# Two PSUM banks for the second attention's projections, and expert outputs added into a stored x by the scatters

## The chip, the cores and the metric

The kernel runs on one core of one Trainium2 chip. The metric is device time in microseconds, lower is better. The kernel before takes 1861.11 us (median of 3 runs, 1853.59 to 1872.67).

## The reference

x has 32 batches of 128 tokens, 256 values each (4096 tokens). Two layers follow one another; each adds an attention and a mixture of experts to x:

```python
x = x + tanh(g_xattn[0]) * L0_xattn(layernorm(x), ctx, ctx, ...)      # 16 heads of 16, with biases
x = x + tanh(g_ffn[0])   * L0_ffn(layernorm(x), ...)                  # 8 experts, top 2, 1024 hidden, relu
x = x + tanh(g_xattn[1]) * L1_xattn(layernorm(x), ctx, ctx, mask)     # causal and padding masks, no W_O
x = x + tanh(g_ffn[1])   * L1_ffn(layernorm(x), ...)                  # 8 experts, top 2, 512 hidden, silu * up
```

In both expert layers a token's output is the sum over its two experts of gate times expert(x). All of it is fp32.

## The kernel before

**Stages.** The program goes through attention 0, experts 0, attention 1, experts 1 and a last combination. x stays in SBUF (tile X) throughout. PE multiplies fp32 as three products of rounded halves (`three`, L371): high by high, high by low, low by high (sources of L373 to L375). So each operand is needed twice: ACT writes the rounded high half and DVE or POOL subtracts it from the whole to get the low half.

**Attention.** Each engine runs its own list in the order of a step counter s, from -21 to 146. A unit is four heads of one batch (128 units); its scores, transposes and products with V sit at fixed steps. A group is four batches (8 groups, 16 steps each). For each group PE also does the transposes of the normalised x ("xt", L416), the projections q, k and v, and for the routing the transposes "lt" (L464), the logits "lg" (L471) and the ranks "rk" (L477, L478). All of these write the one PSUM bank `BK`. `uses_bk` (L323) lists them in order, and `before` makes each wait (`bank_free`, L346) until the one ahead of it has been read out: by DVE for xt, q, k (L755, L763, L773), lg and rk (L797), by ACT for v and lt. The bank `BO_` serves the output projection of attention 0 and is not used in attention 1.

**Routing.** DVE picks two experts per token, their gates (tile GA, times tanh(g_ffn) in tile GT) and the row of each in a memory area sorted by expert. POOL scatters each normalised token twice into `xs_scr` (L1157). A row has 256 values and one more, the number of its place in `ys_scr`: token number plus 4096 for the second choice. Unused rows carry the number 16384.

**Experts.** 39 tiles of 256 rows run per layer, the first 8 of them the first tile of each expert; the number of further tiles per expert is only known on the chip, and tiles left over repeat the last one. Per tile SP fetches rows (L1216) and four parts of weights (L1196) into U1; ACT makes high halves (`act_w`, L650), and POOL (parts 0 and 3) and DVE (parts 1 and 2) the low ones (`low_w`, L1060). PE's order is: up-projection of tile i, transposes of the rows of tile i+1, down-projection of tile i-1. POOL's order per tile (`pool_experts`, L1170) is low half 3 of tile i-1, then `pool_y` of tile i-2, then low half 0 of tile i+1, which the up-projection of tile i+1 needs first. `pool_y` (L1160) waits until the second scatter of the tile before has landed, then issues two indirect DMAs of 128 rows each into `ys_scr` (L1167). In layer 0 DVE adds the bias b2 and writes the output tile `yo` (L1075), in layer 1 ACT copies it (`act_y`, L663). The rows of the next tile are transposed on PE, rounded by ACT (L656) and subtracted by DVE (`dve_turn_x`, L1062); DVE does this after the low halves of the hidden values (L1081 in layer 0, L1083 in layer 1).

**Between the layers and at the end.** `experts_out` (L360) waits for the last scatters. In attention 1 SP loads two outputs per batch from `ys_scr` (L1258) and DVE adds each times its gate to X (L935, L937), ahead of the statistics of the layer norm. After experts 1 SP loads the outputs in 16 DMAs (L1323), DVE does the same sum in 64 instructions (L1356), and ACT's queue writes the result (L1340).

Of the kernel before, what the change touches and what calls it, by code (L numbers as in the profile page):

```python
# [23 lines left out]
ROW = D + 1  # L24
# [20 lines left out]
def constants():  # L45
# [10 lines left out]
    for k in range(2):  # L56
        for b in range(B):
            c[:, C_TOK + k * B + b] = k * T + b * S + p
# [78 lines left out]
def program(nc, A):  # L137
    ctx = ExitStack()
    with ctx:
# [10 lines left out]
        ys_d = [nc.dram_tensor(n, (2 * T, D), F32, kind="Internal").ap() for n in ("ys_scr", "ys1_scr")]  # L150
# [10 lines left out]
        U2 = sb("U2", [128, W0N])  # L161
# [12 lines left out]
        xi = sb("xi", [128, 4, 2], I32)  # L174
        b1s = sb("b1s", [128, 2, 8])
# [19 lines left out]
        GT = sb("GT", [128, 2, 2, B])  # L195
# [30 lines left out]
        YF = [u[:, i * 2048:(i + 1) * 2048].rearrange("p (k g d) -> p k g d", k=2, g=G) for u in (U1, U2, U3) for i in range(2)]  # L226
        YL = U4[:, 0:8 * D].rearrange("p (r k d) -> p r k d", r=4, k=2)
# [6 lines left out]
        oview = A["out"].rearrange("b s d -> s b d")  # L234
# [22 lines left out]
        d_yl = [mark(f"d_yl{r}", [b for b in range(B) if b % 2 == r], 16) for r in range(2)]  # L257
# [8 lines left out]
        d_yf = [mark(f"d_yf{r}", [(g, k) for g in range(NG) if g % 6 == r for k in range(2)], 16) for r in range(6)]  # L266
        d_out = mark("d_out", range(NG), 16)
# [21 lines left out]
        v_yl = mark("v_yl", range(B))  # L289
# [9 lines left out]
        a_y = mark("a_y", [k for k in tile2 if k[0] == 1])  # L299
        m_y = (v_y, a_y)  # L300
# [3 lines left out]
        v_yf = mark("v_yf", range(NG))  # L304
# [35 lines left out]
        before = {}  # L340
# [9 lines left out]
        def banks_out(w, L):  # L350

            w.wait_ge(*a_p[L, NU - 1])
            w.wait_ge(*a_pt[L, NU - 1])
            w.wait_ge(*v_on[L, B - 1])
            w.wait_ge(*a_v[L, NG - 1, 1])
            w.wait_ge(*v_rk[(L,) + PARTS[-1].key])
            if L == 0:
                w.wait_ge(*v_xup[0, B - 1])

        def experts_out(w, L):  # L360

            w.wait_ge(*m_dn[L, NT - 1, 1])
            w.wait_ge(*m_y[L][L, NT - 1, 1])
# [13 lines left out]
        def pe_proj(e, L, wi, src, m):  # L377
            ms = slice(m * 128, m * 128 + 128)
            for t in range(2):
                ins = three(e, BK[:, :], (WR[:, wi, 0, t, ms], WR[:, wi, 1, t, ms]), (src[:, 0, t], src[:, 1, t]), t == 0, t == 1)  # L380
            return ins

        def pe_attention(e, w, L):
            if L == 1:
                experts_out(w, 0)
            for s in range(FIRST, LAST):
# [24 lines left out]
                for t in range(2):  # L411
                    if (g := grp(s, X0[t])) is not None:
                        w.wait_ge(*v_ln1[L, g])
                        bank_free(w, L, "xt", g, t)
                        for j in range(G):
                            ins = e.transpose(BK[:, j * 128:(j + 1) * 128], XN[:, j, t * 128:(t + 1) * 128], ident)  # L416
                        ins.then_inc(*m_xt(L, g, t))
                for m in range(2):
                    if (g := grp(s, Q0[m])) is not None:
# [37 lines left out]
                for p in PARTS:  # L457
                    k = (L,) + p.key
                    for t in range(2):
                        if s == p.lt[t]:  # L460
                            w.wait_ge(*v_xr[k])
                            bank_free(w, L, "lt", p.key, t)
                            for j in range(p.lo, p.hi):
                                ins = e.transpose(BK[:, j * 128:(j + 1) * 128], xr(p.g)[:, 0, j, t * 128:(t + 1) * 128], ident)  # L464
                            ins.then_inc(*m_lt(*k, t))
                    if s == p.e1:
                        w.wait_ge(*a_lt[k + (1,)])
                        bank_free(w, L, "lg", p.key)
                        for j in range(p.lo, p.hi):
                            for t in range(2):  # L470
                                ins = e.matmul(BK[:, j * E:(j + 1) * E], LT[:, t, j * 128:(j + 1) * 128], rw[:, L, t, :], start=t == 0, stop=t == 1)  # L471
                        ins.then_inc(*m_lg(*k))
                    if s == p.rk:
# [3 lines left out]
                        e.matmul(BK[:, 0:p.n * E], cst[:, C_UT:C_UT + 128], sv, start=True, stop=True)  # L477
                        e.matmul(BK[:, 32:32 + p.n * E], cst[:, C_ONE:C_ONE + 128], sv, start=True, stop=True).then_inc(*m_rk(*k))  # L478
# [928 lines left out]
```

## Time and profile before

| what | value |
|---|---|
| runs | 1853.59, 1872.67, 1861.11 us; median 1861.11 |
| profiled execution | 1846.52 us, its span 1844.7 us |
| PE busy | 1653.7 us (90%) |
| weight loads of PE | 1564.0 us (85%) |
| DVE, ACT, POOL busy | 1225.1 (66%), 1198.9 (65%), 791.0 us (43%) |
| mean granted clock of PE | 0.94 |
| DMA | 265.59 MB, 144 GB/s mean |
| chain that ended last | PE 83%, DVE 7%, DMA 3%, issue 2%, POOL 2%, ACT 2% |

Times are us from the start of the span. Attention 0 runs to about 480, experts 0 to 937, attention 1 from about 962 (after the last scatters) to 1438, experts 1 to 1799, the last combination to the end. Busy time of PE is that of modelled matmul ends. "issue" is time in which an engine waited for nothing that the profile shows. A wait is put down to the releaser that came last.

### The profile page before, as it was taken

The numbers are of one execution on the slowest core, as the hardware profiler recorded it, in microseconds if no ns is written. First come the engines' busy times: TensorE is split into PE (matmuls) and PEld (weight loads), VectorE is DVE, ScalarE is ACT, GpSimd is POOL, SyncE is SP. The second block draws the span as 40 slices with busy tenths as digits, with TensorE's granted clock in tenths as the row PEclk, the third lists the DMA queues.
The fourth block names the chain that finished last, engine by engine and source line by source line (L and its number), as shares of the span: only waits on it lengthen the run. The fifth ranks groups of instructions, "written<-read, shape, count | busy, mean of one in ns | idle before, by whom it ended". The sixth has DMA issues, their size and how long they took to land.

```text
span 1844.7 us, 36398 instructions
## 1 busy us (share of the span) xinstructions
PE 1653.7 (90%) x12444; PEld 1564.0 (85%) x12444; DVE 1225.1 (66%) x2877; ACT 1198.9 (65%) x2795; POOL 791.0 (43%) x877
## 2 busy tenths in 40 slices
PE   3999999998599999999976999999995799999990
PEld 2899899897499999999964888888894799999990
DVE  2566665656577777777756677778757566666655
ACT  1667666664488888888843666656662577777760
POOL 2123332224366666666651113333323366666650
PEclk9999998997699999999997999999996799999995
DMA  2212221113677777788742222222221677777758
GB/s 94 47 47 68 66 57 48 48 46 98 168 229 231 231 226 232 229 232 236 225 152 69 63 64 85 79 77 83 57 73 45 206 233 235 230 227 232 231 179 281
DMA packets 209514, 265.59 MB, mean 144 GB/s; under 512 B 28225, under 2 KB 155461, under 8 KB 209201
## 3 DMA queue, kind: packets, MB, share of 16 engines
q1 hardware_dynamic: 189840, 222.36, 41.9%
q0 software_dynamic: 13632, 35.13, 5.2%
q10 hardware_dynamic: 5856, 5.77, 1.0%
q8 instruction: 99, 1.62, 0.4%
q14 instruction: 87, 0.70, 0.1%
HBM read 202.89 MB, written 45.69 MB: 135 GB/s over the span
## 4 chain that ended last, share of the span: by engine, by line
PE 83%; DVE 7%; DMA 3%; issue 2%; POOL 2%; ACT 2%; SPq 1%; DVEq 0%; POOLq 0%; ACTq 0%
PE ps L373 20%; PE ps L375 20%; PE ps L374 20%; PE ps L490 11%; PE ps L393 6%; PE ps L500 2%; PE ps L471 2%; PE ps L409 1%; POOL xs_scr L1157 1%; DMA U<-ys_scr 1%; PE ps L464 1%; PE ps L416 1%; DVE X L1356 1%; DMA xs_scr<-U,PI 1%; DMA ys_scr<-U,xi 1%
## 5 line engine op out<-in xcount | busy, mean ns | idle before, releaser
L1060 POOL TENSOR_TENSOR KXR<-U,KXR 128x1024 fp32r<-128x1024 f32 (+1 forms) x156 | 334.5, 2144 | 306.1 <-ACT KXR L650 305.2
L373 PE MATMUL ps<-QR,KXR 128*128 128x256 f32 x1248 | 355.3, 285 | 8.4 <-DVE QR L1064 8.4
L374 PE MATMUL ps<-QR,KXR 128*128 128x256 f32 x1248 | 354.7, 284 | 0.0
L375 PE MATMUL ps<-QR,KXR 128*128 128x256 f32 x1248 | 354.3, 284 | 0.0
L650 ACT ACTIVATE KXR<-U 128x1024 fp32r<-128x1024 f32 (+1 forms) x312 | 287.7, 949 | 78.0 <-PE ps L375 63.7
L561 ACT ACTIVATE U<-ps,mx 128x128 f32<-128x128 f32 x1024 | 291.7, 379 | 5.7 <-DVE mx L914 5.0
L490 PEld LDWEIGHTS ps<-VA,U 128*128 128x128 f32 x2048 | 267.4, 198 | 9.7
L914 DVE TENSOR_REDUCE mx<-ps 128x4 f32<-128x512 f32 x256 | 175.3, 685 | 126.9 <-PE ps L409 67.3
L490 PE MATMUL ps<-VA,U 128*128 128x17 f32 x2048 | 257.7, 259 | 0.0
L373 PEld LDWEIGHTS ps<-QR,KXR 128*128 128x128 f32 x1248 | 238.6, 191 | 9.7 <-DVE QR L1064 9.7
L374 PEld LDWEIGHTS ps<-QR,KXR 128*128 128x128 f32 x1248 | 238.7, 191 | 0.0
L375 PEld LDWEIGHTS ps<-QR,KXR 128*128 128x128 f32 x1248 | 238.3, 191 | 0.0
L568 ACT ACTIVATE U<-ps 128x512 f32<-128x512 f32 x256 | 157.4, 615 | 60.3 <-PE ps L393 60.1
L1167 POOL DMA_INDIRECT ys_scr<-U,xi x156 | 176.6, 1132 | 40.4 <-issue 35.5
L1060 DVE TENSOR_TENSOR KXR<-U,KXR 128x1024 fp32r<-128x1024 f32 (+1 forms) x156 | 166.6, 1107 | 12.8 <-ACT KXR L650 12.8
L393 PE MATMUL ps<-cst,U 128*128 128x128 f32 x1024 | 166.3, 286 | 0.0
L1157 POOL DMA_INDIRECT xs_scr<-XR,PI x112 | 109.7, 980 | 111.6 <-DVE PI L891 82.9
L1127 POOL TENSOR_TENSOR PTR<-U,PTR 128x1024 fp32r<-128x1024 f32 x16 | 38.0, 2372 | 257.9 <-ACT PTR L573 257.9
L1081 DVE TENSOR_TENSOR PTR<-U,PTR 128x512 fp32r<-128x512 f32 x80 | 109.4, 1386 | 58.4 <-ACT PTR L685 58.4
L674 ACT ACTIVATE U<-ps,b1s 128x256 f32<-128x256 f32 x312 | 130.0, 469 | 17.2 <-PE ps L375 17.1
L373 PE MATMUL ps<-KXR,PTR 128*128 128x256 f32 x480 | 139.2, 290 | 2.2 <-ACT U L663 1.3
L1081 DVE TENSOR_TENSOR WR<-U,WR 128x512 fp32r<-128x512 f32 x76 | 107.3, 1433 | 49.1 <-ACT WR L685 49.1
(191 smaller groups left out, 4024.4 us busy)
## 6 DMA issues: line engine op xcount, KB each, us to landing
U<-in_wpack SPq DMA_DIRECT2D x234, 512.0 KB, 4.1
U<-xs_scr SPq DMA_DIRECT2D x78, 257.0 KB, 4.4
U<-in_wpack SPq DMA_DIRECT2D x78, 256.0 KB, 3.5
KXR<-U SPq DMA_DIRECT2D x512, 32.0 KB
U<-in_ctx_t SPq DMA_DIRECT2D x16, 512.0 KB, 3.9
U<-ys_scr SPq DMA_DIRECT2D x32, 256.0 KB, 2.9
U<-ys_scr SPq DMA_DIRECT2D x16, 512.0 KB, 10.0
XR<-in_L_ffn_b SPq DMA_DIRECT2D x39, 128.0 KB, 3.9
```

The lines of the kernel that those rows point to most:

```text
L373: e.matmul(o, wh, xh, start=first, stop=False)
L374: e.matmul(o, wh, xl, start=False, stop=False)
L375: return e.matmul(o, wl, xh, start=False, stop=done)
L393: ins = e.transpose(bank[:, h * 128:(h + 1) * 128], PB[:, i % 3, h], ident)
L490: ins = e.matmul(OB[:, hh * 17:(hh + 1) * 17], PT[:, i % 3, h], VA[:, v, j % 2, hh, :], start=True, stop=True)
L561: ins = e.activation(PB[:, i % 3, h], SB_[i % 3][:, h * 128:(h + 1) * 128], ACT.Exp, bias=mx[:, i % 4, h:h + 1], scale=-1.0)
L568: e.activation(PT[:, i % 3].rearrange("p h k -> p (h k)"), PTB[i % 2][:, :], ACT.Copy).then_inc(*a_pt(L, i))
L650: e.activation(w_cols(L, WH, n), w_raw(L, n), ACT.Copy).then_inc(*a_w[n](L, i))
L914: e.tensor_reduce(mx[:, i % 4], SB_[i % 3][:, :].rearrange("p (h k) -> p h k", h=4), AX.X, ALU.min).then_inc(*v_mx(L, i))
L1060: e.tensor_tensor(w_cols(L, WL, n), w_raw(L, n), hi, ALU.subtract).then_inc(*l_w[n](L, i))
L1081: ins = e.tensor_tensor(low[:, 2 * q:2 * q + 2], HB[:, i % 2, 2 * q:2 * q + 2], high[:, 2 * q:2 * q + 2], ALU.subtract)
L1167: e.indirect_dma_start(ys_d[L], bass.IndirectOffsetOnAxis(ap=xi[:, i % 4, a:a + 1], axis=0), yo[:, r, a, :], None, bounds_check=2 * T - 1, ...
```

## The change

1. **Banks.** In layer 1 `place` gives the users of the bank `BK` and `BO_` in turn, and each waits for the one two ahead of it. In layer 0 it stays one bank.
2. **x in memory.** After each attention SP stores X by groups of four batches (512 KB each): in layer 0 into a scratch `x1_scr`, in layer 1 into the output itself. SP loads group by group from `x1_scr` at the start of attention 1 and beside it.
3. **Gates in the rows.** A scattered row has 258 values: also the gate times tanh(g_ffn). The tile GT is gone. The place number is the token number alone, for both choices.
4. **ScalarE applies the gate.** `act_y` now runs in both layers, as a copy with a scale per row. In layer 0 it works in place on `yo` after DVE's addition of b2, and stands behind the second quarter of the hidden values.
5. **Scatters add.** `pool_y` scatters with an addition in the DMA into the stored x. It waits for the landing of the scatter before it (as before), and for tile 0 for the last store of x. Tiles left over get numbers out of bounds, by an instruction on DVE that makes `su`, and are not written.
6. **Gone:** the loads from `ys_scr` and the additions L935, L937 in attention 1, and the whole last combination.

```diff
-ROW = D + 1
+ROW = D + 2
-                c[:, C_TOK + k * B + b] = k * T + b * S + p
+                c[:, C_TOK + k * B + b] = b * S + p
-        ys_d = [nc.dram_tensor(n, (2 * T, D), F32, kind="Internal").ap() for n in ("ys_scr", "ys1_scr")]
+        sum_d = [nc.dram_tensor("x1_scr", (T, D), F32, kind="Internal").ap(), A["out"].rearrange("b s d -> (b s) d")]
...
         for L in LL:
-            uses = uses_bk(L)
-            for (_, empty), (use, _) in zip(uses, uses[1:]):
+            uses, nb = uses_bk(L), L + 1
+            for (_, empty), (use, _) in zip(uses, uses[nb:]):
                 before[(L,) + use] = empty
+            for n, (use, _) in enumerate(uses):
+                place[(L,) + use] = (BK, BO_)[n % nb]
...
-        def act_y(e, w, i):
-            w.wait_ge(*m_dn[1, i, 1])
-            if i >= 2:
-                w.wait_ge(*d_fy[i % 2][1, i - 2, 1])
+        def act_y(e, w, L, i):
+            w.wait_ge(*v_xi[L, i])
+            if L == 0:
+                w.wait_ge(*v_y[0, i, 1])
+            else:
+                w.wait_ge(*m_dn[1, i, 1])
+                if i >= 2:
+                    w.wait_ge(*d_fy[i % 2][1, i - 2, 1])
             for a in range(2):
-                e.activation(yo[:, i % 2, a], YB[a][:, 0:D], ACT.Copy).then_inc(*a_y(1, i, a))
+                y = YB[a][:, 0:D] if L else yo[:, i % 2, a]
+                e.activation(yo[:, i % 2, a], y, ACT.Copy, scale=xg[:, i % 4, a:a + 1]).then_inc(*a_y(L, i, a))
...
                 for q in range(4):
                     act_hidden(e, w, L, i, q)
+                    if L == 0 and q == 1 and i >= 2:
+                        act_y(e, w, 0, i - 2)
...
-            e.tensor_scalar(GT[:, L, :, p.bs], GA[:, L, :, p.bs], th[:, 2 + L:3 + L], None, ALU.mult).then_inc(*v_ga(*k))
+            e.tensor_scalar(xr(p.g)[:, :, p.js, D + 1:D + 2].rearrange("p z g o -> p z (g o)"), GA[:, L, :, p.bs], th[:, 2 + L:3 + L], None, ALU.mult).then_inc(*v_ga(*k))
...
-                            e.scalar_tensor_tensor(X[:, b], YL[:, b % 2, 0], GT[:, 0, 0, b:b + 1], X[:, b], ALU.mult, ALU.add).then_inc(*v_c.up())
-                            w.wait_ge(*v_c.now)
-                            e.scalar_tensor_tensor(X[:, b], YL[:, b % 2, 1], GT[:, 0, 1, b:b + 1], X[:, b], ALU.mult, ALU.add).then_inc(*v_yl(b))
...
+            e.tensor_scalar(su[:, :], ti, tl[:, 2, E - 1:E], float(4 * T), ALU.is_gt, ALU.mult).then_inc(*v_c.up())
...
-            e.tensor_copy(xi[:, i % 4], xt[:, i % 2, :, D]).then_inc(*v_xi(L, i))
+                w.wait_ge(*a_y[L, i - 4, 1])
+            e.tensor_copy(xg[:, i % 4], xt[:, i % 2, :, D + 1]).then_inc(*v_c.up())
+            if i < E:
+                ins = e.tensor_copy(xi[:, i % 4], xt[:, i % 2, :, D])
+            else:
+                if i == E:
+                    w.wait_ge(*v_tl[L])
+                ins = e.tensor_scalar(xi[:, i % 4], xt[:, i % 2, :, D], su[:, i - E:i - E + 1], None, ALU.add)
+            ins.then_inc(*v_xi(L, i))
...
             w.wait_ge(*v_xi[L, i])
-            if i:
-                w.wait_ge(*d_fy[1 - r][L, i - 1, 1])
+            w.wait_ge(*(d_fy[1 - r][L, i - 1, 1] if i else d_xs[L, NG - 1]))
             for a in range(2):
-                w.wait_ge(*m_y[L][L, i, a])
-                e.indirect_dma_start(ys_d[L], bass.IndirectOffsetOnAxis(ap=xi[:, i % 4, a:a + 1], axis=0), yo[:, r, a, :], None,
-                                     bounds_check=2 * T - 1, oob_is_err=False).then_inc(*d_fy[r](L, i, a))
+                w.wait_ge(*a_y[L, i, a])
+                e.indirect_dma_start(sum_d[L], bass.IndirectOffsetOnAxis(ap=xi[:, i % 4, a:a + 1], axis=0), yo[:, r, a, :], None,
+                                     bounds_check=T - 1, oob_is_err=False, compute_op=ALU.add).then_inc(*d_fy[r](L, i, a))
...
-        def sp_load_x(e, g):
-            e.dma_start(X[:, g * G:(g + 1) * G, :], xin[:, g * G:(g + 1) * G, :]).then_inc(*d_x[g](g))
+        def sp_load_x(e, L, g):
+            e.dma_start(X[:, g * G:(g + 1) * G, :], (xin, sview[0])[L][:, g * G:(g + 1) * G, :]).then_inc(*(d_x, d_xl)[L][g](g))
...
                 experts_out(w, 0)
+                sp_load_x(e, 1, 0)
...
+                if (g := grp(s, 41)) is not None:
+                    w.wait_ge(*v_xup[L, (g + 1) * G - 1])
+                    e.dma_start(sview[L][:, g * G:(g + 1) * G, :], X[:, g * G:(g + 1) * G, :]).then_inc(*d_xs(L, g))
...
             experts_out(w, 1)
-            ysv = ys_d[1].rearrange("(k b p) d -> p k b d", k=2, p=128)
-            for g in range(NG):
-                if g >= 6:
-                    w.wait_ge(*v_yf[g - 6])
-                for k in range(2):
-                    e.dma_start(YF[g % 6][:, k], ysv[:, k, g * G:(g + 1) * G]).then_inc(*d_yf[g % 6](g, k))
+            w.wait_ge(*d_xs[1, NG - 1])
...
-            for g in range(NG):
-                w.wait_ge(*v_yf[g])
-                e.dma_start(oview[:, g * G:(g + 1) * G, :], X[:, g * G:(g + 1) * G, :]).then_inc(*d_out(g))
...
-                        e.scalar_tensor_tensor(X[:, b], YF[g % 6][:, k, j], GT[:, 1, k, b:b + 1], X[:, b], ALU.mult, ALU.add)
```

## Rows read from the trace of the kernel before

**Rows 1.** Busy time by stage: stretch, length, engines, clock, DMA share, GB/s.

```profile
482.00:937.00 455.00, 450.07 (x3756) 449.46 (x3757) 348.13 (x377) 374.05 (x646) 276.86 (x147) 0.99 0.78 228
985.00:1438.00 453.00, 401.64 (x2708) 358.56 (x2708) 319.37 (x1020) 266.14 (x755) 123.09 (x265) 0.93 0.26 73
1438.00:1798.00 360.00, 354.59 (x2956) 353.78 (x2957) 222.85 (x467) 260.75 (x582) 215.65 (x152) 0.98 0.71 222
1798.00:1844.70 46.70, 1.17 (x10) 0.97 (x9) 26.41 (x64) 0.66 (x2) 2.92 (x3) 0.56 0.82 278
```

**Rows 2.** Chain that ended last, after 1796 us: start, length, what.

```profile
1798.25 2.32 DMA ys_scr<-U,xi
...
1802.66 2.29 DMA ys_scr<-U,xi
...
1838.08 1.68 DVE X L1356 x4
```

**Rows 3.** DMA issues, whole span: KB each, median us to landing.

```profile
U<-ys_scr SPq DMA_DIRECT2D x32, 256.0 KB, 2.9
```

**Rows 4.** POOL in order of time, end of layer 0: start, length, idle before.

```profile
956.89 0.97 POOL L1167 DMA_INDIRECT ys_scr<-U,xi  x1 [2.22 <-DVE U L1075]
```

**Rows 5.** PE waits, 985 to 1001 us: total us, times, longest.

```profile
PE ps L373 <- DVE QR L763: 2.9, 2, 1.5
PE ps L416 <- DVE PTR L755: 1.4, 1, 1.4
```

**Rows 6.** PE waits, 1001 to 1385 us.

```profile
PE ps L373 <- DVE RK L797: 7.4, 5, 1.7
PE ps L477 <- DVE U L773: 4.4, 3, 1.5
PE ps L373 <- DVE QR L763: 3.6, 7, 0.5
```

**Rows 7.** Groups of DVE instructions, 985 to 1438 us: busy, mean ns, idle.

```profile
L935 DVE SCALAR_TENSOR_TENSOR X<-U,GT,X 128x256 f32<-128x256 f32 x28 | 26.1, 932 | 0.0
...
L937 DVE SCALAR_TENSOR_TENSOR X<-U,GT,X 128x256 f32<-128x256 f32 x28 | 13.6, 485 | 1.0
```

**Rows 8.** ACT in order of time, one expert tile of layer 0.

```profile
702.91 0.84 ACT L674 ACTIVATE U<-ps,b1s 128x256 f32<-128x256 f32 x2
...
711.95 1.06 ACT L650 ACTIVATE KXR<-U 128x1024 fp32r<-128x1024 f32 x1 [1.57 <-PE ps L375]
```

**Rows 9.** POOL in order of time, the same tile.

```profile
703.84 1.26 POOL L1167 DMA_INDIRECT ys_scr<-U,xi  x1 [0.16 <-issue]
...
706.80 2.42 POOL L1060 TENSOR_TENSOR KXR<-U,KXR 128x1024 fp32r<-128x1024 f32 x1
```

**Rows 10.** DVE in order of time, the same tile.

```profile
706.64 3.74 DVE L1081 TENSOR_TENSOR PTR<-U,PTR 128x512 fp32r<-128x512 f32 x2 [0.70 <-ACT PTR L685]
710.30 0.68 DVE L1064 TENSOR_TENSOR QR<-ps,QR 128x512 fp32r<-128x512 f32 x1
```

**Rows 11.** PE in order of time, the first matmul of the next tile.

```profile
711.69 0.28 PE L373 MATMUL ps<-QR,KXR 128*128 128x256 f32 x1
```

**Rows 12.** POOL in order of time, one expert tile of layer 1.

```profile
1602.24 2.44 POOL L1060 TENSOR_TENSOR KXR<-U,KXR 128x1024 fp32r<-128x1024 f32 x1
```

**Rows 13.** PE in order of time, first matmul of the next tile.

```profile
1606.07 0.28 PE L373 MATMUL ps<-QR,KXR 128*128 128x256 f32 x1
```

**Rows 14.** Groups of POOL instructions, 500 to 930 us.

```profile
L1167 POOL DMA_INDIRECT ys_scr<-U,xi x71 | 92.4, 1301 | 16.4 <-issue 16.1
```

**Rows 15.** Groups of POOL instructions, 1450 to 1790 us.

```profile
L1167 POOL DMA_INDIRECT ys_scr<-U,xi x73 | 71.9, 984 | 17.0 <-issue 17.0
```

**Rows 16.** DMA queues and issues, 600 to 900 us.

```profile
q0 software_dynamic: 2465, 5.70, 5.0%
...
ys_scr<-U,xi POOLq DMA_INDIRECT x51, 4.7
```

**Rows 17.** DMA queues and issues, 1500 to 1700 us.

```profile
ys_scr<-U,xi POOLq DMA_INDIRECT x45, 4.0
```

More of the change, by code:

```diff
@@ L174, in program @@
         xi = sb("xi", [128, 4, 2], I32)
+        xg = sb("xg", [128, 4, 2])
+        su = sb("su", [128, NT - E])
         b1s = sb("b1s", [128, 2, 8])
@@ L233, in program @@
         ident = cst[:, C_ID:C_ID + 128]
-        oview = A["out"].rearrange("b s d -> s b d")
+        sview = [v.rearrange("(b p) d -> p b d", p=128) for v in sum_d]
         xin = A["x"].rearrange("b s d -> s b d")
@@ L298, in program @@
         m_dn, v_y = mark("m_dn", tile2), mark("v_y", [k for k in tile2 if k[0] == 0])
-        a_y = mark("a_y", [k for k in tile2 if k[0] == 1])
-        m_y = (v_y, a_y)
+        a_y = mark("a_y", tile2)
         a_w = [mark(f"a_w{n}", tiles) for n in range(4)]
@@ L470, in pe_attention @@
                             for t in range(2):
-                                ins = e.matmul(BK[:, j * E:(j + 1) * E], LT[:, t, j * 128:(j + 1) * 128], rw[:, L, t, :], start=t == 0, stop=t == 1)
+                                ins = e.matmul(place[L, "lg", p.key][:, j * E:(j + 1) * E], LT[:, t, j * 128:(j + 1) * 128], rw[:, L, t, :], start=t == 0, stop=t == 1)
                         ins.then_inc(*m_lg(*k))
@@ L476, in pe_attention @@
                         sv = SEL[:, p.js].rearrange("p g e -> p (g e)")
-                        e.matmul(BK[:, 0:p.n * E], cst[:, C_UT:C_UT + 128], sv, start=True, stop=True)
-                        e.matmul(BK[:, 32:32 + p.n * E], cst[:, C_ONE:C_ONE + 128], sv, start=True, stop=True).then_inc(*m_rk(*k))
+                        e.matmul(place[L, "rk", p.key][:, 0:p.n * E], cst[:, C_UT:C_UT + 128], sv, start=True, stop=True)
+                        e.matmul(place[L, "rk", p.key][:, 32:32 + p.n * E], cst[:, C_ONE:C_ONE + 128], sv, start=True, stop=True).then_inc(*m_rk(*k))
                 if 0 <= s - 2 < NU:
@@ L519, in pe_down @@
             if i:
-                w.wait_ge(*m_y[L][L, i - 1, 1])
+                w.wait_ge(*(a_y if L else v_y)[L, i - 1, 1])
             for f in range(nf):
@@ L578, in act_attention @@
                             w.wait_ge(*m_q[L, g - 1, 1])
-                        e.activation(XT[:, 0, t], BK[:, :], ACT.Copy).then_inc(*a_xt(L, g, t))
+                        e.activation(XT[:, 0, t], place[L, "xt", g, t][:, :], ACT.Copy).then_inc(*a_xt(L, g, t))
                 for m in range(2):
@@ L758, in dve_rests @@
                     w.wait_ge(*a_q[L, g, m])
-                    hi, lo = QR[:, g % 2, 0, m].bitcast(F32), QR[:, g % 2, 1, m]
+                    hi, lo, bank = QR[:, g % 2, 0, m].bitcast(F32), QR[:, g % 2, 1, m], place[L, "q", g, m]
                     if L == 0:
-                        ins = e.scalar_tensor_tensor(lo, BK[:, :], bqk[:, 0, m:m + 1], hi, ALU.add, ALU.subtract)
+                        ins = e.scalar_tensor_tensor(lo, bank[:, :], bqk[:, 0, m:m + 1], hi, ALU.add, ALU.subtract)
                     else:
-                        ins = e.tensor_tensor(lo, BK[:, :], hi, ALU.subtract)
+                        ins = e.tensor_tensor(lo, bank[:, :], hi, ALU.subtract)
                     ins.then_inc(*v_q(L, g, m))
@@ L940, in dve_attention @@
                         b = g * G + j
-                        w.wait_ge(*(v_yl[b] if L else d_x[g][g]))
+                        w.wait_ge(*(d_xl if L else d_x)[g][g])
                         e.bn_stats(st6[:, 0, j], X[:, b]).then_inc(*v_c.up())
@@ L1348, in _ @@
                 dve_experts(e, w, L)
-            for g in range(NG):
-                for k in range(2):
-                    w.wait_ge(*d_yf[g % 6][g, 1])
-                    if k:
-                        w.wait_ge(*v_c.now)
-                    for j in range(G):
-                        b = g * G + j
-                        ins = e.scalar_tensor_tensor(X[:, b], YF[g % 6][:, k, j], GT[:, 1, k, b:b + 1], X[:, b], ALU.mult, ALU.add)
-                        if j == G - 1:
-                            ins.then_inc(*(v_yf(g) if k else v_c.up()))
         @block.tensor
```

77 lines of the change are left out of this document (30 added, 47 removed).

## The prediction

> **What bounds the kernel now.** I read the busy time by stage first. In both expert stages PE is busy for all but 5 us (450.07 of 455, 354.59 of 360), with ACT at 82% and 72% [rows 1]. Attention 1 is also a PE stage, but with holes: 401.64 of 453. The last stage, 46.7 us, has hardly any PE: it is the combination [rows 1]. The chain of waits shows that stage bare: scatter lands, sums on DVE, output [rows 2]. So an edit pays if it takes time out of the end, out of the boundary between the layers, or out of PE's holes in attention 1. It costs if it delays what PE needs next in one of the 78 expert tiles.
>
> **The end.** The last scatter starts at 1802.66 and lands 2.29 us later, at 1804.95 [rows 2]. All behind it goes: 1844.7 - 1804.95 = **39.8 us**. The stores of x that replace it lie in the attentions, where the DMA share is 0.26 [rows 1]. One store per group of about 50 us waits on SP for DVE's update of X, at a step later than that update; the next K copies behind it on SP's queue wait for later scores anyway. Cover gone, each of the 16 stores would cost about an issue, 1.0 us by POOL's [rows 15], 16 us in all.
>
> **Slower landings at the end.** An adding scatter reads its destination and then writes. The trace has no such DMA. Below: nothing, if read and write of different rows overlap. Above: a whole read of such outputs, 2.9 us [rows 3]. A gain is excluded, since each row still is written. I take the middle, 1.5 us. At the end of layer 1 two scatters follow each other, each tile's waiting for the one before (2.32 and 2.29 us, [rows 2]): **+3.0**, bounds 0 and 5.8.
>
> **End of layer 0.** DVE's last sum releases the scatter at 956.89 [rows 4]. Now ACT's copy stands between (0.84 us for two with a per-partition operand, [rows 8], so 0.4 for the first), then one slower landing, and the tile before it may be late by some tenths: **+2.5**, bounds 0.4 and 6.
>
> **Start of attention 1.** DVE no longer adds eight outputs to the first group ahead of its statistics, 0.49 to 0.93 us each [rows 7]. But DVE also had weights to scale and a wait for the first K projection, so I count only 1.5. The load of x (512 KB, issued first) is hidden behind that weight work. Then comes a chain xt, xt, q, q, v, v, in which one bank makes PE wait for every reading out: 2.9 and 1.4 us [rows 5], to which I add 0.7 for v (an estimate, half of the smaller). With two banks PE writes the second while the first is read: 5.0 less, of which the first scores may give back a little. Together **-6**, bounds 0 and -8.
>
> **Steady part of attention 1.** PE waits for the release of the bank by RK 7.4, by K's low half 4.4, by Q's 3.6 us [rows 6], 15.4 in all. Two things work on them. The bank two uses back is nearly always free; and DVE, which releases it late, loses 26.1 + 13.6 = 39.7 us of work [rows 7]. Nothing else stands behind these waits: DVE's busy share falls from 0.71 to 0.62, ACT's is 0.59 [rows 1]. **-13**, bounds 0 and -15.4. Late next is PE itself.
>
> **The tail of attention 1** stays: with one group left its routing is a serial chain on DVE and eight scatter issues on POOL, which no second bank shortens. The new `su` instruction comes before the tile list, needed only at tile 8: 0.
>
> **Expert tiles of layer 0.** A tile takes 455 / 39 = 11.7 us. ACT gets 0.84 us more per tile. It has a hole of 1.57 us per tile, waiting for PE [rows 8], so its sum still fits: 9.6 + 0.84 of 11.7. But order counts. POOL's scatters now wait for ACT's copy, which starts when the second quarter is done (702.91 + 0.84) and gives the first half at about 704.2; they began at 703.84 [rows 9]. So POOL's low half for the next tile moves from 706.80 to about 707.2. While POOL runs it, DVE stands: its two low halves of the hidden values take 3.74 us and end 1.1 us after POOL's instruction; then 0.68 for the rows of the next tile, done at 710.98 [rows 9, 10]. PE wants them at 711.69 [rows 11]. Margin 0.7, less 0.4 to 0.6: it just holds. DVE's additional tiny instructions come behind it. I take **+2** over 39 tiles for tiles in which it doesn't; bounds 0 and, with 0.3 us lost per tile, 12.
>
> **The rings.** In layer 0 an issue takes POOL 1301 ns, in layer 1 984 ns [rows 14, 15], and it is layer 0 where DVE reads and writes SBUF all the time. The Trainium skill (DMA: Bandwidth & Descriptors, SWDGE vs HWDGE vs iDMA) says that these descriptors are written by GpSimd into SBUF, and that DVE can lock it out. By that rule an adding scatter with more descriptors would suffer most in layer 0; the price of that is a rival below.
>
> **Expert tiles of layer 1.** ACT's copy exists already. POOL's low half ends at 1604.68, PE needs it at 1606.07 [rows 12, 13]: 1.4 us for slower issues. **0**.
>
> **DMA.** The scatters' queue takes 5.0% of the 16 engines in layer 0, whose share is 0.78 [rows 1, 16]. Doubled, that is 0.83: no bound.
>
> **Sum.** -39.8 + 3.0 + 2.5 - 6 - 13 + 2 = **-51.3 us**. The profiled execution took 1846.52 (span 1844.7), 14.6 below the median shown, so 1795 for such an execution and 1861.1 - 51.3 = **1810** as a median.
>
> **Rivals.**
>
> *A. Landings set the tile (slower).* POOL waits for the second scatter of the tile before. In layer 1 the limit from its issue to its landing is a tile less one issue and gap: 9.2 - 1.3 = 7.9 us; it takes 4.0 now [rows 15, 17]. In layer 0 it is 11.7 - 1.6 = 10.1 against 4.7 [rows 14, 16]. Beyond it POOL can't start the low half, and PE waits. With y us more per landing the cost is 3y at the ends plus 39 (y - 3.9) in layer 1. Gross gain 56.8: the change turns slower from y = 5, a landing of 9 us. At 9.5 us it costs 16 + 62 + 4 = 82, so 1861 - 57 + 82 = 1886. For it: nothing here shows reads that must end before writes. Against: it would take more than two present landings in a row. POOL's issue can do the same: doubled (1.3 and 1.0 us more) it costs 39 x (2.6 - 0.9) in layer 0 and 39 x (2.0 - 1.4) in layer 1, 90 us, so about 1900. 0.11 for both.
>
> *B. Issues half as long again.* 0.65 us more in layer 0, two per tile. The order then frees 0.6 of DVE's tail, since its third low half slips ahead of POOL; with the 0.3 of margin left that gives 39 x (1.3 - 0.9) = 16 us, layer 1 nothing: 1826. 0.13.
>
> *C. Landings double.* In layer 1 8.0 us, just at its limit (+2), and the ends cost 8 and 5 instead of 3 and 2.5: 1810 + 10 = 1820. The queue's share of 5.0% doubles without harm [rows 16]. The Trainium skill (Collectives: The Full Stack, The bandwidth ceiling) says that a reducing transfer needs two source reads and runs at half the rate of a copy. No DMA of this trace adds, so it cannot agree or disagree. 0.12.
>
> *D. The holes in attention 1 don't close.* If PE only waits a little later, for scores, exponentials or DVE's chain, the -19 shrinks to -9: 1820. Against: DVE and ACT idle a third of that stage. 0.09.
>
> *E. Some sum near nothing*, two of these together or a tile of layer 0 longer by a microsecond (+39): 1849. 0.06.
>
> The rest, 0.49, is the forecast. That it doesn't do what it says is hardly possible for the end: the instructions are gone.
>
> **Range.** Low: -39.8 - 15.4 - 8 + 0.4 = -63, 1798; less the half spread of the runs, 1790. High: B, C, D and part of E, 1850. Outside: A, half of E and a little below. Within 1% is 1842 to 1880, about what a measurement can tell from no change here. Faster 0.81, same 0.07, slower 0.12.
>
> **What would show it.** Right: the span ends 1 to 3 us after the last scatter; attention 1 some 19 us shorter, with PE's waits for RK and the low halves of K and Q under 4 us; tiles of 11.7 and 9.2 us with PE busy throughout. Wrong: PE idle ahead of the up-projection's first matmul, released by POOL's or DVE's low half; POOL's scatters released by the DMA before them in every tile; an issue well over 1.3 us; landings over 7 us.

## The result and the profile after

The changed kernel takes **1879.64 us** (median of 20 runs, 1866.93 to 1903.57), the kernel before beside it 1858.28 (20 runs): ratio 1.0111, 95% interval 1.0081 to 1.0141. It is slower by 1.1%; 1810 was predicted. Two later comparisons gave 1.0139 (1.0071 to 1.0208) and 1.0140 (1.0069 to 1.0211).

The profiled execution took 1876.88 us, its span 1875.1. Busy time by stage, same columns as [rows 1]:

```profile
490.00:1026.00 536.00, 475.60 (x3755) 467.44 (x3754) 417.86 (x412) 405.36 (x718) 314.06 (x147) 0.96 0.74 193
1074.00:1496.00 422.00, 392.00 (x2706) 356.21 (x2705) 281.13 (x965) 265.83 (x755) 124.05 (x265) 0.94 0.29 79
1496.00:1862.00 366.00, 359.33 (x2952) 355.98 (x2953) 243.31 (x506) 271.56 (x582) 260.58 (x152) 0.98 0.79 217
1862.00:1875.10 13.10, 1.70 (x15) 1.50 (x13) 0.00 (x0) 0.84 (x2) 5.52 (x4) 0.65 0.03 2
```

The last stage is 13 us instead of 47 and attention 1 is 31 us shorter, as meant. But expert stage 0 is 81 us longer for the same 3755 matmuls: PE idles 60 us of it, where it idled 5, and its busy time is 26 us longer.

To compare kernels I cut each trace at PE's transposes of rows (one set per expert tile): start to first tile; the 38 tile periods of layer 0; last tile of layer 0 to first of layer 1; layer 1; the tail. Us, from one profiled execution each; "tile" is the mean of tiles 8 to 30:

| kernel | start | experts 0 | between | experts 1 | tail | span | tile 0 | tile 1 |
|---|---|---|---|---|---|---|---|---|
| before | 482.1 | 448.8 | 507.6 | 344.2 | 62.0 | 1844.7 | 11.86 | 9.00 |
| changed | 489.7 | **530.3** | 476.0 | 351.0 | 28.1 | 1875.1 | **14.26** | 9.14 |
| changed again, after2 | 478.2 | 527.5 | 493.8 | 351.3 | 28.2 | 1879.0 | 14.12 | 9.17 |
| changed again, after3 | 475.5 | 530.7 | 497.0 | 351.6 | 28.1 | 1882.9 | 14.22 | 9.20 |
| POOL's order turned, swap0c | 483.4 | 449.2 | 493.6 | 348.9 | 28.1 | 1803.3 | 11.86 | 9.12 |

Changed less before: +7.6 +81.5 -31.6 +6.8 -33.9 = +30.4 us. The start differs from execution to execution (489.7 at a granted clock of 0.89, 478.2 and 475.5 at 0.92), so its +7.6 is not put down to the change.

PE's waits in experts 0 (total us, times, longest), changed, 488 to 1028 us:

```profile
PE ps L371 <- DVE QR L1064: 60.4, 38, 3.4
```

and before, 482 to 937 us:

```profile
PE ps L373 <- DVE QR L1064: 4.8, 2, 3.4
```

"Split" is the subtraction that gives the low half. DVE's split of the next tile's rows was late twice, in the first two tiles; now it is late there and again in every tile from the fourth on, by 0.7 to 2.7 us. This is the sign that the prediction gave for "wrong". One tile of the changed kernel in order of time (start, length, idle before and its releaser), first POOL:

```profile
710.85 2.96 POOL L1060 TENSOR_TENSOR KXR<-U,KXR 128x1024 fp32r<-128x1024 f32 x1
715.06 3.48 POOL L1060 TENSOR_TENSOR KXR<-U,KXR 128x1024 fp32r<-128x1024 f32 x1 [1.26 <-ACT KXR L649]
721.77 1.55 POOL L1174 DMA_INDIRECT x_scr<-U,xi  x1 [3.23 <-ACT U L668]
723.63 1.55 POOL L1174 DMA_INDIRECT x_scr<-U,xi  x1 [0.30 <-issue]
724.62 2.99 POOL L1060 TENSOR_TENSOR KXR<-U,KXR 128x1024 fp32r<-128x1024 f32 x1
```

then DVE:

```profile
710.68 3.69 DVE L1089 TENSOR_TENSOR WR<-U,WR 128x512 fp32r<-128x512 f32 x1 [0.70 <-ACT WR L690]
714.29 0.68 DVE L1064 TENSOR_TENSOR QR<-ps,QR 128x512 fp32r<-128x512 f32 x1
...
715.09 4.53 DVE L1060 TENSOR_TENSOR KXR<-U,KXR 128x1024 fp32r<-128x1024 f32 x2
719.54 0.74 DVE L1083 TENSOR_TENSOR U<-ps,XR 128x256 f32<-128x256 f32 x2
```

and ACT:

```profile
705.49 0.91 ACT L668 ACTIVATE U<-U,xg 128x256 f32<-128x256 f32 x2 [1.38 <-DVE U L1083]
```

Read together, this is a ring. (1) POOL's scatters wait for the gate (L668), and the low half for the next tile stands behind them (724.62). (2) While it runs (one tile earlier, 710.85) DVE stands: a split of 0.69 takes 3.69 (710.68), the split of the rows comes at 714.29, and PE waits. (3) POOL's other low half (715.06) now falls on DVE's two low halves of weights (715.09), which take 4.53. (4) So the sum with the bias (719.54) is late, the gate on ACT waits for it, and the scatters of the next tile are late too. The ring has a second way back: SP fetches the next weights into the raw buffer only after POOL's low half has read it, and ACT then waits for that DMA. Before, ACT never waited for it in experts 0; now:

```profile
ACT KXR L649 <- DMA U<-in_wpack: 34.3, 26, 2.6
```

How the delay divides over the two ways is not separated here. A late landing is no part of it: POOL's list waits for the landing of the tile before, but in the changed kernel every scatter of layer 0 but the last tile's starts 3.5 us or more after that landing (4.1 before). The tile periods are not even: 12.9, 14.4 and 15.9 us follow one another irregularly (12.8 to 16.4 from the fourth on), where nearly all were 11.82 to 11.90 before.

### The profile page after: what moved, and what is told of

It reads as the page before. It is cut to its first block, busy times and chain, and to the rows that moved or that the text cites. A ratio compares the mean times of both kernels' runs of the same rounds, so it can differ in the third digit from the quotient of the medians.

```text
span 1875.1 us, 36500 instructions
## 1 busy us (share of the span) xinstructions
PE 1683.9 (90%) x12444; PEld 1591.3 (85%) x12444; DVE 1248.6 (67%) x2829; ACT 1243.9 (66%) x2873; POOL 880.7 (47%) x877
## 4 chain that ended last, share of the span: by engine, by line
PE 62%; DVE 17%; ACT 8%; issue 7%; POOL 2%; DMA 2%; SPq 0%; POOLq 0%; DVEq 0%; ACTq 0%
PE ps L371 14%; PE ps L373 13%; PE ps L372 13%; PE ps L489 10%; PE ps L391 6%; DVE KXR L1060 5%; DVE PTR L1089 3%; DVE WR L1089 2%; ACT U L679 2%; ACT KXR L649 2%; PE ps L470 1%; DVE QR L1064 1%; PE ps L407 1%; POOL xs_scr L1165 1%; ACT U L668 1%
## 5 line engine op out<-in xcount | busy, mean ns | idle before, releaser
L1060 POOL TENSOR_TENSOR KXR<-U,KXR 128x1024 fp32r<-128x1024 f32 (+1 forms) x156 | 395.3, 2534 | 213.1 <-ACT KXR L649 210.4
L371 PE MATMUL ps<-QR,KXR 128*128 128x256 f32 x1248 | 369.8, 296 | 66.3 <-DVE QR L1064 64.0
L372 PE MATMUL ps<-QR,KXR 128*128 128x256 f32 x1248 | 362.3, 290 | 0.0
L373 PE MATMUL ps<-QR,KXR 128*128 128x256 f32 x1248 | 361.9, 290 | 0.0
L371 PEld LDWEIGHTS ps<-QR,KXR 128*128 128x128 f32 x1248 | 246.7, 198 | 77.8 <-DVE QR L1064 72.8
L560 ACT ACTIVATE U<-ps,mx 128x128 f32<-128x128 f32 x1024 | 292.5, 380 | 14.4 <-DVE mx L920 14.4
L372 PEld LDWEIGHTS ps<-QR,KXR 128*128 128x128 f32 x1248 | 246.9, 198 | 0.0
L373 PEld LDWEIGHTS ps<-QR,KXR 128*128 128x128 f32 x1248 | 246.7, 198 | 0.0
L1060 DVE TENSOR_TENSOR KXR<-U,KXR 128x1024 fp32r<-128x1024 f32 (+1 forms) x156 | 215.8, 1421 | 4.4 <-ACT KXR L649 4.1
L1174 POOL DMA_INDIRECT x_scr<-U,xi x78 | 122.1, 1565 | 116.3 <-ACT U L668 99.0
L1089 DVE TENSOR_TENSOR PTR<-U,PTR 128x512 fp32r<-128x512 f32 x80 | 116.8, 1478 | 60.2 <-ACT PTR L690 60.2
L1089 DVE TENSOR_TENSOR WR<-U,WR 128x512 fp32r<-128x512 f32 x76 | 115.6, 1540 | 58.8 <-ACT WR L690 58.8
```

Of the source, the lines that this page charges most:

```text
L371: e.matmul(o, wh, xh, start=first, stop=False)
L372: e.matmul(o, wh, xl, start=False, stop=False)
L373: return e.matmul(o, wl, xh, start=False, stop=done)
L560: ins = e.activation(PB[:, i % 3, h], SB_[i % 3][:, h * 128:(h + 1) * 128], ACT.Exp, bias=mx[:, i % 4, h:h + 1], scale=-1.0)
L1060: e.tensor_tensor(w_cols(L, WL, n), w_raw(L, n), hi, ALU.subtract).then_inc(*l_w[n](L, i))
L1089: ins = e.tensor_tensor(low[:, 2 * q:2 * q + 2], HB[:, i % 2, 2 * q:2 * q + 2], high[:, 2 * q:2 * q + 2], ALU.subtract)
```

## The experiments

Four groups of runs were timed, each beside the kernel before: swap0, plain0, nogate0, neither0; then swapboth, onebank, banks, after2; then swap0b, plain1, early0, dvegate0; then pad0, swap0c, after3. In the first and third group the kernel before took 1925.06 and 1922.80 us, in the others 1853.57 and 1857.36. By the profiles of one kernel in two groups most of the longer time lies ahead of the first expert tile: 528.6 us in swap0 and 483.4 in swap0c. The granted clock (0.89 and 0.90) explains some 12 us of it; the rest is open. So medians are compared within a group only. Kernels that leave something out, and early0 and dvegate0, were run once.

### Which part makes the tile longer

**swap0**: POOL's order turned, in layer 0 only.

```diff
+                if L == 0 and i + 1 < NT:
+                    low_w(e, w, L, i + 1, 0)
                 if i >= 2:
                     pool_y(e, w, L, i - 2)
-                if i + 1 < NT:
+                if L == 1 and i + 1 < NT:
                     low_w(e, w, L, i + 1, 0)
```

> After the change a tile of layer 0 takes 13 to 16 us (530 us from the first tile's transposes to the last's) where it took 11.8 (449 us). Here POOL makes the low half for tile i+1 before it issues the scatters of tile i-2, in layer 0 alone; nothing is left out. Theory 'queue' (POOL's low half stands behind scatters that now wait for ACT and take longer to issue): tiles go back to 11.8 to 12.1 us, the run is 65 to 85 us below the changed kernel, about 1800. Theory 'landing or DMA' (adding scatters load the DMA engines or land late and hold everything): the tiles stay over 13 us and the run within 20 us of the changed kernel.

**plain0**: scatters of layer 0 overwrite (the sum is left out), gate as changed.

```diff
-    bounds_check=T - 1, oob_is_err=False, compute_op=ALU.add)
+    bounds_check=T - 1, oob_is_err=False, **({'compute_op': ALU.add} if L else {}))
```

> The changed kernel, but the scatters of layer 0 overwrite instead of adding, so layer 1 works on other values. ACT's gating stays. If the adding itself is the cause (longer issues on POOL, or landings), tiles of layer 0 go back to under 12.3 us; if ACT's copy ahead of the scatters is, they stay at 13 us or more. I expect about half: 12.3 to 13.3 us.

**nogate0**: in layer 0 the gate is left out; the scatters add, and wait for DVE's sum.

```diff
-                    if L == 0 and q == 1 and i >= 2:
-                        act_y(e, w, 0, i - 2)
...
-                w.wait_ge(*a_y[L, i, a])
+                w.wait_ge(*m_y[L][L, i, a])
```

> The changed kernel, but ACT doesn't apply the gate in layer 0 (the scatters add ungated rows as soon as DVE has added b2). Adding stays. If ACT's place ahead of the scatters is the cause, tiles go back to under 12.3 us; if the adding is, they stay at 13 us or more. I expect 11.9 to 12.6 us, since POOL begins 1.5 us earlier.

**neither0**: both edits.

> The changed kernel with neither gate nor adding in layer 0 (ungated rows overwrite). Every theory that names one of the two expects the tile of before, 11.8 to 11.9 us. If it stays above 12.3, the cause is a third thing, as DVE's additional small instructions or the wider rows.

Measured: tile of layer 0 and experts 0, then the time.

| layer 0 has | tile | experts 0 | time |
|---|---|---|---|
| neither | 11.86 | 449.7 | 1841.72 |
| gate only (plain0) | 12.17 | 459.2 | 1854.09 |
| adding only (nogate0) | 12.59 | 474.5 | 1865.06 |
| both (changed) | 14.26 | 530.3 | 1876.88 |
| both, order turned (swap0) | 11.86 | 448.7 | 1845.71, ratio to before 0.9593 (0.9547 to 0.9638) |

Alone the parts cost 0.3 and 0.7 us per tile, together 2.4, more than twice their sum. Part of the 2.4 is granted clock. Tiles 8 to 30, 22 periods, same columns as [rows 1]; before, plain0, nogate0 and changed in this order:

```profile
575.10:836.00 260.90, 260.90 (x2203) 260.90 (x2201) 204.29 (x221) 216.79 (x375) 164.59 (x89) 1.00 0.79 231
```

```profile
615.50:883.30 267.80, 266.01 (x2202) 262.37 (x2201) 224.24 (x242) 234.46 (x419) 177.02 (x89) 1.00 0.77 225
```

```profile
612.40:889.20 276.80, 266.53 (x2202) 262.11 (x2200) 235.26 (x242) 214.07 (x372) 186.96 (x89) 1.00 0.82 217
```

```profile
593.80:907.50 313.70, 278.59 (x2203) 274.12 (x2201) 247.90 (x242) 237.47 (x421) 188.92 (x89) 0.96 0.76 195
```

In the changed kernel PE idles 35 us of these, 1.6 per tile; a clock of 0.956 costs 14 us, 0.6 per tile; 0.2 are left. Without the clock it is 1.8 against 0.3 + 0.7. (The time of the changed kernel is from another group, the other four from one; swap0 is a median of four runs.) With POOL's order turned, gate and adding are both there and the tile is that of before: POOL has the low half done before the ring can close. In order of time, swap0c:

```profile
702.96 2.38 POOL L1060 TENSOR_TENSOR KXR<-U,KXR 128x1024 fp32r<-128x1024 f32 x1 [1.37 <-ACT KXR L649]
707.27 2.40 POOL L1060 TENSOR_TENSOR KXR<-U,KXR 128x1024 fp32r<-128x1024 f32 x1 [1.92 <-ACT KXR L649]
709.82 1.82 POOL L1174 DMA_INDIRECT x_scr<-U,xi  x1 [0.15 <-issue]
```

```profile
707.74 3.68 DVE L1089 TENSOR_TENSOR PTR<-U,PTR 128x512 fp32r<-128x512 f32 x3 [1.84 <-ACT PTR L690]
711.34 0.68 DVE L1064 TENSOR_TENSOR QR<-ps,QR 128x512 fp32r<-128x512 f32 x1
711.94 0.20 DVE L1068 COPY xg<-U 128x2 f32<-128x2 f32 x1
712.06 0.22 DVE L1074 TENSOR_SCALAR xi<-U,su 128x2 int32<-128x2 f32 x1
712.19 2.35 DVE L1060 TENSOR_TENSOR KXR<-U,KXR 128x1024 fp32r<-128x1024 f32 x2
```

The low half at 707.27 now ends at 709.67, ahead of DVE's next pair, which takes 2.35 instead of 4.53.

### Issue or landing

**pad0**: plain0, and POOL clears a tile that nobody reads before each scatter of layer 0.

```diff
+                if L == 0:
+                    e.memset(pdw[:, :], 0.0).then_inc(*p_c.up())
+                    w.wait_ge(*p_c.now)
```

> The changed kernel with scatters of layer 0 that overwrite instead of adding (the sum of layer 0 is wrong in it: this part of the computation is left out), and ahead of each of them POOL clears a tile of 128x320 floats that nobody reads, by my estimate 0.3 to 0.45 us, which holds POOL about as long as an adding scatter does. Theory POOL: only the time that POOL is held matters. Then the tile of layer 0 goes from 12.17 us (overwriting, no hold) to 13.5 to 14.5, with PE idle behind DVE's split rows as in the changed kernel, and the stage from 459 to 515 to 540 us. Rival landing: the later landings of an adding scatter and their load on the queues make the difference. Then the tile stays under 12.5 and the stage under 470.

Tile 14.33 us, experts 0 534.3. Groups of POOL's instructions (count, busy, mean ns, idle), 600 to 900 us, pad0:

```profile
L1178 POOL DMA_INDIRECT x_scr<-U,xi x42 | 50.0, 1190 | 34.0 <-POOL pdw L1176 31.8 <-issue 2.2
L1176 POOL MEMSET pdw<- 128x320 f32 x41 | 15.3, 372 | 50.2 <-ACT U L669 50.1
```

changed:

```profile
L1174 POOL DMA_INDIRECT x_scr<-U,xi x42 | 65.6, 1561 | 63.4 <-ACT U L668 53.1 <-issue 10.3
```

plain0:

```profile
L1174 POOL DMA_INDIRECT x_scr<-U,xi x50 | 56.3, 1126 | 25.7 <-ACT U L668 17.5 <-issue 8.3
```

1190 + 372 = 1562 ns, as long as an adding issue, and the tile is that of the changed kernel, without any adding (one run, 1872.30 us). But the wait on the clearing adds 0.8 us of idle time per scatter, so POOL is held about twice as long over plain0 as the adding holds it. So a hold of POOL can bring this tile about without adding transfers; that a hold of the adding's own size would do so by itself is not shown. What speaks against the transfers in the changed kernel is that no scatter of layer 0 waited for a landing (above), and that swap0 has the same transfers and the tile of before.

### Two ways to bring the gate forward

**early0**: the gate after the first quarter of the hidden values (`q == 0` for `q == 1`). **dvegate0**: nogate0, and DVE multiplies by the gate after its sum.

> The changed kernel in its own order of POOL, but ACT applies the gate behind the first quarter of the hidden values instead of the second, 1.4 us earlier. Theory 'queue': the tile of layer 0 depends on when POOL gets to its low half, so it falls from 14.2 to between 12.6 (no gate at all) and 13.5 us. If the gate's share is only ACT's own time, it stays near 14.2.

> The changed kernel with DVE applying the gate in layer 0 (two instructions of about 0.35 us more per tile on DVE, none on ACT); nothing is left out, POOL's order is that of the change. POOL's scatters start 0.7 us later than without a gate instead of 2.5. Theory 'queue' expects 12.9 to 13.6 us per tile; if ACT's load were the matter, 12.6 as without gate.

early0 (1925.07 us, one run): tile 13.94, where 12.6 to 13.5 was expected, so hardly any help: the gate cannot start before DVE's sum. ACT's waits:

```profile
ACT U L668 <- DVE U L1083: 50.9, 27, 2.8
```

dvegate0 (1901.30 us, one run): tile 13.04, stage 490.1, as the reading by POOL's queue expected. It takes back half of the 2.4 us; POOL's order took back all.

### Layer 1, the banks, and the size of it all

**swapboth**: the low half ahead in both layers. **onebank**: swap0 with `uses, nb = uses_bk(L), 1`. **banks**: the kernel before with `uses_bk(L), L + 1` and `place`, and the one wait ahead of the experts that the second bank needs. **plain1**: swap0, and the scatters of layer 1 overwrite (the sum is left out). **after2**, **after3**: the changed kernel. **swap0b**, **swap0c**: swap0.

> POOL makes the low half for tile i+1 ahead of the scatters in both layers; nothing is left out. In layer 1 the changed kernel's tiles take 9.1 to 9.2 us where they took 9.0 before. Theory 'queue' expects 9.0 again, some 5 us below the version that swaps in layer 0 alone, so 4.2 to 4.5% under the kernel before. If the slower tiles of layer 1 come from the DMA engines (their share is 0.81 where it was 0.71), they stay at 9.1 to 9.2.

> The version that swaps in layer 0, but with one bank in layer 1 as before; x still comes from memory and DVE's additions are gone. From the last tile's transposes of layer 0 to the first's of layer 1 it was 507.6 us before and 476.0 after the change (-31.6). If the banks give most of it, this stays near 505 on the same clock; if DVE's freed time gives most, it is near 485. I expect the halves to be about equal: 14 to 18 us more than with two banks.

> The kernel before with the second bank in layer 1 alone. The stretch between the expert stages gets 12 to 20 us shorter than before (my forecast had 18 us from PE's waits), all else stays, so a ratio to the kernel before of about 0.991 to 0.994. If DVE's additions are what holds the attention, it gains under 6 us.

> The same version, but the scatters of layer 1 overwrite the output rows instead of adding. If the adding DMAs are what makes the tiles of layer 1 9.13 to 9.25 us where they took 9.00, they go back to 9.0 and the scatters' queue from 17% of the DMA engines to about 7%. If it is ACT's copy with a scale (0.84 us for two, 0.66 before) or DVE's small instructions, they stay.

> The version that swaps POOL's order in layer 0 alone, again, for its ratio to the kernel before on a chip of the usual clock. In the first comparison it was 0.959 on a chip whose attentions were slow; on one where the kernel before takes 1853 to 1861 us I expect 0.968 to 0.977: 31 us of clock-free attention, 34 us of tail, less 6 us in layer 1 and what the granted clock takes back.

> The changed kernel with POOL's low half for the next tile ahead of the scatters, layer 0 only; timed beside the kernel before and the changed kernel. Theory order: tile of layer 0 11.86 us as in the kernel before, ratio to the kernel before 0.972 to 0.980 where that takes its usual 1855 us (0.96 where it takes 1923), and 0.955 to 0.97 of the changed kernel. Rival clock: part of what the order gives is taken back in the attentions by lower granted clock, ratio 0.985 or more.

> The changed kernel itself, on the same chip as the others, with nothing altered. Expected: about 1.1% above the kernel before as in the first comparison, tiles of layer 0 between 13 and 16 us. On a chip whose attentions run at a lower clock the ratio can come out lower, since its gains lie in the attentions and its loss in the expert tiles of layer 0.

> The changed kernel once more, as the neighbour of the repaired one. Theory order: 1.008 to 1.018 of the kernel before, 25 to 33 us above ... the kernel before plus 20 to 30 us, tile of layer 0 at 14.1 to 14.3 us. Rival (its slowness was due to the state of that chip): within 0.5% of the kernel before, tile at 12.5 or less.

| kernel | time | ratio to before (95%) | between | tile 0 | tile 1 |
|---|---|---|---|---|---|
| banks | 1841.70 | 0.9932 (0.9896 to 0.9969) | 494.4 | 11.86 | 9.00 |
| onebank | 1812.18 | 0.9763 (0.9707 to 0.9819) | 504.3 | 11.86 | 9.13 |
| swapboth | 1813.86 | 0.9763 (0.9711 to 0.9815) | 498.8 | 11.86 | 9.25 |
| swap0c | 1807.87 | 0.9768 (0.9713 to 0.9823) | 493.6 | 11.86 | 9.12 |
| swap0b | 1849.12 | 0.9605 (0.9566 to 0.9644) | 501.4 | 11.86 | 9.16 |
| plain1 | 1835.03 | (one run) | 499.6 | 11.86 | 9.00 |

**swap0c** beats both kernels: 2.3% under the kernel before, and in the same group 75.5 us under the changed kernel (1883.38, after3). In the profiles of the two experts 0 is 81.5 us shorter.

In layer 1 the scatters that add cost 0.12 to 0.25 us per tile in these kernels; with overwriting ones it is 9.00 again (plain1). The queue of the scatters and their landing, changed, 1650 to 1850 us (packets, MB, share of the 16 engines; then count and median us):

```profile
q0 software_dynamic: 6336, 4.97, 17.2%
...
out<-U,xi POOLq DMA_INDIRECT x44, 5.3
```

and plain1, 1600 to 1800 us:

```profile
q0 software_dynamic: 2121, 5.08, 6.5%
```

An adding scatter takes 2.7 times the DMA time per MB, in three times the packets. The loads of the weights feel it. ACT's waits for them in layer 1, before, changed and plain1:

```profile
ACT KXR L650 <- DMA U<-in_wpack: 0.3, 1, 0.3
```

```profile
ACT KXR L649 <- DMA U<-in_wpack: 11.7, 29, 1.2
```

```profile
ACT KXR L649 <- DMA U<-in_wpack: 1.3, 3, 0.7
```

Whether these waits, the longer issues or the landings make up the 0.14 us was not separated. Turning the order in layer 1 brought nothing (9.25, where 9.0 was one forecast and 9.1 to 9.2 the other). There the scatters come later, and the landing becomes late, for POOL in nearly every tile and for DVE; swapboth, layer 1:

```profile
DVE xg L1068 <- DMA out<-U,xi: 41.5, 31, 2.4
```

The changed kernel has no such wait.

### The clock takes part of attention 1 back

Attention 1 from its first product with V to its last, the same work in every kernel; same columns as [rows 1]; before, changed, swap0c, swapboth and banks in this order, each fence one kernel:

```profile
1011.90:1399.30 387.40, 372.03 (x2585) 336.42 (x2583) 277.78 (x843) 249.46 (x713) 101.92 (x243) 0.98 0.25 70
```

```profile
1096.10:1459.70 363.60, 363.34 (x2585) 333.28 (x2583) 242.80 (x796) 249.33 (x713) 102.16 (x239) 0.99 0.29 76
```

```profile
1007.10:1389.20 382.10, 381.85 (x2584) 349.40 (x2583) 242.72 (x793) 249.30 (x713) 102.24 (x239) 0.94 0.28 72
```

```profile
1015.20:1402.20 387.00, 386.71 (x2584) 353.31 (x2583) 242.87 (x793) 248.75 (x713) 102.09 (x239) 0.93 0.27 71
```

```profile
1010.90:1391.40 380.50, 376.63 (x2585) 342.33 (x2583) 274.92 (x843) 248.69 (x713) 103.44 (x243) 0.96 0.26 71
```

| kernel | length | PE idle | granted clock | length times clock |
|---|---|---|---|---|
| before | 387.4 | 15.4 | 0.976 | 378.1 |
| onebank | 381.7 | 9.8 | 0.972 | 371.0 |
| banks | 380.5 | 3.9 | 0.958 | 364.5 |
| changed | 363.6 | 0.3 | 0.991 | 360.3 |
| after2 | 378.9 | 0.2 | 0.947 | 358.8 |
| after3 | 380.8 | 0.3 | 0.942 | 358.7 |
| swap0c | 382.1 | 0.2 | 0.939 | 358.8 |
| swapboth | 387.0 | 0.3 | 0.926 | 358.4 |

PE's holes are gone (0.3 us idle instead of 15.4). The last column is an estimate of the length at full clock. By it the second bank alone is worth 14 us here, DVE's relief alone 7, both 18 to 20, in all five executions alike. What differs is the granted clock: 0.99 in the changed kernel's first profile, and 0.93 to 0.95 in the other four that have both parts. A mean of 0.94 over 382 us is 46 us at the lower level (1.2 GHz), 23 us lost; 0.93 over 387 is 27 to 29 us lost, and swapboth is as long there as the kernel before. The changed kernel itself differs by just this: "between" is 476.0 in one execution, 493.8 and 497.0 in two others. In these PE idles hardly at all, and before, with holes, the clock was at 0.98. But only one execution of the kernel before was profiled, so that filled holes lower the clock is suggested and not shown.

## Why the prediction was wrong

- **The end** (-39.8 + 3.0 = -36.8): -33.9. The landing grew by only 0.41 us (2.73 against 2.32), where I took 1.5. The error is in "all behind it goes": the last scatter starts at 1868.58 and the span ends 6.5 us after that, where 2.3 and the slower landing stood, and the last scatter comes 1.6 us later after the last tile's transposes (21.6 against 20.0 us), with issues 0.6 us longer. The chain near the end:

```profile
1861.30 1.56 POOL out L1174
...
1863.17 2.73 DMA out<-U,xi
...
1866.72 1.55 POOL out L1174
```

- **End of layer 0, attention 1** (+2.5 - 6 - 13 = -16.5): -31.6 in the profile of the result, -13.8, -10.6, -14.0 and -8.8 in four others (after2, after3, swap0c, swapboth). The mechanism held: of the 15.4 us of waits in [rows 6] 0.2 is left. In the profile of the result the part up to the first product with V gave 4.9 us (3.5 were expected), the steady part 23.8 (13 were expected), the part behind it 2.9 (0). The size depends on the clock, which the prediction left out: at full clock the steady part is worth 18 to 20 us by the table above, and the clock took up to all of it back. That this profile shows -31.6 and the others -9 to -14 is luck of its clock.
- **Expert tiles of layer 0** (+2, bounds 0 and 12): **+81.5. This is the step that failed**: "Margin 0.7, less 0.4 to 0.6: it just holds", and "with 0.3 us lost per tile, 12". Three things were wrong in it. First, the margin took the wait for the gate (0.4 to 0.6) and not the longer issues, which I priced as a rival by themselves; in swap0c, without the ring, they are 1692 ns against 1301, two of them 0.8 us. Together that is 1.2 to 1.4 us, above the margin of 0.7. The gate did more than this wait, too: in plain0 POOL waits 0.7 us for it (24.8 us in 36 tiles), but DVE's split of the rows ends 6.3 us after the tile's transposes instead of 5.4. ACT rounds the rows 0.8 us later there, behind its gate, and POOL's low halves last 2.90 us instead of 2.44. Second, the bound was linear: it counted how late the rows come and not that a late POOL meets DVE's next instructions too, which delays its own release. An excess of 0.5 to 0.7 us became 1.8 without the clock (plain0 with 0.3, nogate0 with 0.7 and both together show that it is no sum, and swap0's 11.86 that it goes through POOL's order). Third, the granted clock: 0.954 for 0.988 between the first and last tile's transposes is 24 less 5 us lost, about 19 of the 81; PE's additional waits are 56 (60.4 - 4.8). The other 7 are not accounted for. That the waits lower the clock is not shown: over the 22 periods above nogate0 with 10 us of idle PE and dvegate0 with 19 of 287 have 1.00, the changed kernel with 35 has 0.956.
- **Rows 14 and 15**, the issue: an adding one is 1556 ns in layer 1 against 984 (+58%), in layer 0 1561 to 1692 against 1301 (+20 to 30%), or, with the same order around it, 1561 against 1126 (plain0) and 1692 against 1240 (neither0), +36 to 39%. The rule from the Trainium skill (DMA: Bandwidth & Descriptors, SWDGE vs HWDGE vs iDMA), that DVE can lock GpSimd's descriptor writes out, made me expect the larger growth in layer 0; it grew more in layer 1. The page ties this to DVE's 2-port perf mode, and no view here tells DVE's mode. The trace agrees with it only in that a plain issue is slower beside DVE, 1301 against 984.
- **Rivals.** A: no landing sets the tile of layer 0 (each scatter starts 3.5 us or more after the landing it waits for); its second form, issues doubled, gave the right size (90 us) for a growth that was not there. B had the right mechanism, longer issues, even at half the size (0.39 us for 0.65), but 16 us for it: the same linear sum, and without the gate's delay. C: landings went from 4.0 to 5.3, not 8.0; the queue's DMA time per MB went up 2.7 times in layer 1. The Trainium skill (Collectives: The Full Stack, The bandwidth ceiling) has a reducing transfer at half the rate of a copy. The trace of these small rows shows less than half, by the 2.7. D did not happen.
- **Expert tiles of layer 1** (0): +6.8. PE isn't held by POOL's low half there; adding costs 0.14 us per tile, since plain1 has 9.00 again.
- With +2 in place of +81.5 the sum would be -49 instead of -51 in this execution; the repaired kernel gave -41 in its profile.

## What to carry to other kernels

When two small delays go into one margin, add all of them, the duration of the instruction as well as its wait, before calling the margin held; and when the delayed engine stalls the one that releases it, ask what it collides with next: past the margin the cost can be a multiple of the excess, as here. Put what the next tile needs first ahead of anything that waits for the last tile's result; turning two calls was worth 75 us here. When holes of TensorE are filled, read the granted clock beside the holes, in more than one execution.

## What the runs showed of the hardware

- An indirect scatter with addition, 128 rows of 256 floats: issue 1556 ns on POOL against 984 for the overwriting one (layer 1); landing alone 2.73 us against 2.32, under load 5.3 against 4.0; 2.7 times the DMA time per MB, three times the packets.
- A DVE instruction with two SBUF operands stands while POOL computes in SBUF: 0.69 us becomes 3.69, and a pair of 2.35 becomes 4.53. POOL's own grows too, from 2.4 to 3.0 or 3.5.
- The granted clock behaved in two ways: in the expert stage it is 1.00 while PE never idles (swap0c, all of 600 to 800 us), and between 0.93 and 1.00 in the changed kernel's stretches of 40 to 50 us, with a gap of 0.7 to 2.7 us in each tile; in attention 1, PE never idle either, it is 0.93 to 0.99. What tells the two stages apart was not tried.
